# Moving the first context's rounding, the last softmax sums and the first tile's gates in a one-core pre-norm attention layer

## The reference, cut to what matters

```
h = x + attention(layernorm(x))        # 16 heads of 32, rotary q and k, causal softmax, output weights Wo
out = h + ffn(layernorm(h))
ffn(x) = x @ base_w.T + base_b + 2 * sum_e gate[e] * (x @ lora_A[e]) @ lora_B[e]   # 8 experts of rank 16
gate: softmax(x @ router_w.T + router_b), the two highest kept and divided by their sum
```

## Time and profile before

| | |
|---|---|
| median of three runs | 1532.85 us (1532.79 to 1534.3) |
| the profiled execution's own time | 1535.1 us |
| its span, first to last instruction | 1533.4 us |
| PE busy | 1503.7 us, 98% |
| DVE busy | 1134.1 us, 74% |
| ACT busy | 756.0 us, 49% |
| POOL busy | 890.6 us, 58% |
| PE's share of the chain that ended last | 91% |

### The profile page before, as it was taken

How to read it: one execution, slowest core, us unless ns; L and a number is a source line. 1 busy time by engine, 2 the same in 40 slices (tenths; PEclk the granted TensorE clock), 3 DMA queues, 4 the chain that set the end, 5 groups by cost and what they waited for, 6 DMA issues and landing times.

```text
span 1533.4 us, 24788 instructions
## 1 busy us (share of the span) xinstructions
PE 1503.7 (98%) x9056; PEld 978.2 (64%) x9056; DVE 1134.1 (74%) x2277; ACT 756.0 (49%) x1540; POOL 890.6 (58%) x597
## 2 busy tenths in 40 slices
PE   6999999999999999999999999999999989999999
PEld 5888888755555555555555555555555547777777
DVE  6766666899777877778777777877777677666665
ACT  3222222155666656657666666666665673233221
POOL 2333233567778778788788787887797721121111
PEclk9999999999999999999999999999999999999999
DMA  6656685858359457467566665754845363223411
GB/s 206 213 186 211 201 259 186 226 129 191 77 112 193 91 125 180 87 137 166 111 131 141 137 136 115 164 118 107 191 101 132 85 153 112 82 83 101 138 63 55
DMA packets 120403, 215.83 MB, mean 141 GB/s; under 512 B 12504, under 2 KB 45784, under 8 KB 113112
## 3 DMA queue, kind: packets, MB, share of 16 engines
q1 hardware_dynamic: 102384, 136.20, 32.7%
q0 software_dynamic: 8064, 58.72, 18.7%
q10 hardware_dynamic: 9840, 19.40, 3.5%
HBM read 96.23 MB, written 58.72 MB: 101 GB/s over the span
## 4 chain that ended last, share of the span: by engine, by line
PE 91%; DVE 4%; DMA 3%; issue 1%; ACT 0%; POOL 0%; SPq 0%; DVEq 0%; POOLq 0%; ACTq 0%
PE a_mx L275 17%; PE a_st L1029 17%; PE a_av L1042 16%; PE p_pair L533 11%; PE f_wo_ps L1393 5%; PE f_out_ps L1453 5%; PE p_v L545 5%; PE a_sum L275 3%; PE a_sum L1064 2%; PE a_sum L1072 2%; PE f_out_ps L1468 1%; PE f_mid_ps L1393 1%; DVE a_part L290 1%; PE a_mx L279 1%; PE f_tr_ps L1412 1%; DMA a_gather<-a_pair 1%
## 5 line engine op out<-in xcount | busy, mean ns | idle before, releaser
L1130 ACT ACTIVATE a_probs<-a_st 128x512 f32<-128x512 f32 (+2 forms) x1244 | 573.7, 547 | 344.2 <-PE a_st L1029 338.8
L290 DVE TENSOR_REDUCE a_part<-a_mx 128x1 f32<-128x512 f32 (+1 forms) x766 | 490.1, 679 | 81.7 <-PE a_mx L275 72.3
L978 POOL TENSOR_TENSOR a_pair<-a_probs 128x1024 f32<-128x1024 f32 (+2 forms) x224 | 401.4, 1832 | 18.8 <-DMA a_gather<-a_pair 6.5
L978 POOL TENSOR_TENSOR a_gather<-a_probs 128x1024 f32<-128x1024 f32 x76 | 180.0, 2388 | 94.8 <-ACT a_probs L1130 94.8
L407 POOL TENSOR_TENSOR p_rot<-p_mul 128x1024 f32<-128x1024 f32 x32 | 87.5, 2735 | 193.9 <-DVE p_mul L711 193.9
L1386 POOL TENSOR_TENSOR f_x<-f_x,f_bias 128x512 f32<-128x512 f32 x32 | 40.2, 1291 | 201.6 <-DVE f_xn L1606 201.6
L1042 PE MATMUL a_av<-a_probs,a_v 128*32 128x512 f32 (+3 forms) x1280 | 139.8, 537 | 2.3 <-POOL a_probs L959 2.3
L1042 PE MATMUL a_av<-a_probs,shared 128*32 128x512 f32 (+3 forms) x1280 | 140.1, 537 | 0.0
L293 DVE CUSTOM_DVE_ANT_0 a_mx<-a_mx,f_ctx 128x512 f32<-128x512 f32 (+1 forms) x161 | 98.5, 630 | 52.2 <-PE a_mx L275 52.2
L959 POOL TENSOR_SCALAR_AFFINE_SELECT a_probs<-a_probs 128x512 f32<-128x512 f32 x128 | 88.9, 759 | 54.8 <-ACT a_probs L1130 52.2
L1029 PE MATMUL a_st<-a_q_stack,a_k_stack 98*128 98x512 f32 (+3 forms) x287 | 101.6, 371 | 1.1 <-DMA a_q_stack<-a_neg_rows 1.1
(11 more groups left out here) (241 smaller groups left out, 3036.2 us busy)
## 6 DMA issues: line engine op xcount, KB each, us to landing
a_gather<-a_pair POOLq DMA_DIRECT2D x56, 1024.0 KB, 7.1
qk_scratch<-p_rot_hi SPq DMA_DIRECT2D x32, 512.0 KB, 3.1
qk_scratch<-p_rot_lo SPq DMA_DIRECT2D x32, 512.0 KB, 3.9
a_k_stack<-qk_scratch SPq DMA_DIRECT2D x60, 256.0 KB, 8.1
a_q_first<-qk_scratch SPq DMA_DIRECT2D x48, 256.0 KB, 6.0
a_third<-qk_scratch SPq DMA_DIRECT2D x36, 256.0 KB, 5.4
v_scratch<-p_v_st SPq DMA_DIRECT2D x32, 256.0 KB, 7.0
ctx_scratch<-a_ctx_st SPq DMA_DIRECT2D x32, 256.0 KB, 2.7
```

Of the source, the lines that this page charges most:

```text
L290: dve.tensor_reduce(found, scores.rearrange("p (h n) -> p h n", n=width), AX.X, ALU.max).then_inc(self.max_done, 1)
L978: pool.tensor_tensor(place[:, h:h + 2, q0:TT], probs[:, s % RING, h:h + 2, q0:TT], probs[:, (s + 1) % RING, h:h + 2, q0:TT], ALU.add).then ...
L1130: act.activation(probs[:, s % RING, h, q0:TT], score_bank(g, HG * s + h)[:, q0:TT], ACT.Exp, scale=SCORE_SCALE).then_inc(exp_done, 1)
```

## The change

The first context is rounded at pair 11 of the last group instead of pair 17, right behind that pair's addition. SP waits for the last join of either gather buffer before it loads the second context. PE does the sums of pair 19 behind output product 0, and waits there for the rounded output weights. In `finish` DVE does the second addition and the router weights' remainders before the second context's part; the lora_a weights' roundings and remainders come after the root and the norm. In tile 0 the logits are turned after 4 of the 12 matmuls of `down`, and the next tile's additions 0 and 1 follow the gates instead of preceding them.

```
--- before.py
+++ after.py
@@ -90,7 +90,6 @@
 ITEM_END = [max(n for n, it in enumerate(ITEMS) if it[0] == t) for t in range(QT)]
 HEAD_START = NITEM // 2 + 5
 BEFORE_FIRST = ITEM_END[1] + 1
-SPLIT_FROM = NPAIR - 7
 SHIFTS = 16 * 4
 IN_PAIRS = 5
 ITEM_AFTER = [24 * p + 4 * n + 7 for p in range(4) for n in range(IN_PAIRS)]
@@ -120,6 +119,7 @@
 
 UNIT_READY = [LAST_PAIR[t] - 1 for t in range(QT - 1)]
 OPENING = 6
+SPLIT_AT = {LAST_PAIR[2]: KT, **{LAST_PAIR[2] + 2 + n: n for n in range(KT)}}
 
 
 def items_before(p, first):
@@ -934,6 +934,8 @@
             sp.dma_start(early.x0[:, :, :], early.x_v[0]).then_inc(early.x_loaded[0], 16)
             group(GROUPS - 1, 1, False, True)
             sp.wait_ge(early.c_lo_done, 1 + START)
+            for a in range(2):
+                sp.wait_ge(gather_joined[a], 16 * joined(NPAIR * GROUPS - 1, a))
             sp.dma_start(early.cin, early.ctx_v[0, :, :, TT:2 * TT]).then_inc(early.ctx_loaded, 16)
 
         def store_last(sp):
@@ -1092,8 +1094,10 @@
                                     scores(g + 1, 1 - par, s - NSTEP, h)
                         for half in steps:
                             values(g, par, 2 * p + half)
-                    sums(g, p)
-
+                    if not (last and p == NPAIR - 1):
+                        sums(g, p)
+
+            early.last_sums = lambda: sums(GROUPS - 1, NPAIR - 1)
             pe.wait_ge(first.mul_done, 4 * TILES + PROJECT_AHEAD)
             for n in range(2 * HG):
                 scores(0, 0, n // HG, n % HG)
@@ -1159,13 +1163,12 @@
 
             def split_early(n):
 
-                if n == 0:
-                    dve.wait_ge(st_done, HG * NSTEP * (GROUPS - 1))
                 if n < KT:
                     dve.wait_ge(early.w_loaded[n], 16)
                     raw, hi, lo = early.w_raw[:, n, :], early.wo_hi[:, n, :], early.wo_lo[:, n, :]
                     hi_done, lo_done, count = early.w_hi_done, early.w_lo_done, n + 1
                 else:
+                    dve.wait_ge(st_done, HG * NSTEP * (GROUPS - 1))
                     dve.wait_ge(early.ctx_loaded, 16)
                     raw, hi, lo = early.cin, early.c_hi, early.c_lo
                     hi_done, lo_done, count = early.c_hi_done, early.c_lo_done, 1
@@ -1191,8 +1194,8 @@
                 for p in range(NPAIR):
                     if last and p >= NO_ITEMS:
                         add_pair(g, p)
-                    if last and SPLIT_FROM <= p <= SPLIT_FROM + KT:
-                        split_early(p - SPLIT_FROM)
+                    if last and p in SPLIT_AT:
+                        split_early(SPLIT_AT[p])
                     items = [(n, k) for n, k in items_of_pair(p, opening) if not (n and last)]
                     ended = [(g - before, t) for before, t in unit_ended_before(p, 1) if not (before and opening)]
                     for unit in ended:
@@ -1398,6 +1401,8 @@
                 m = 4 * T + s
                 if s == 0:
                     pe.wait_ge(c_lo_done, T + 1 + START)
+                if m == 0:
+                    pe.wait_ge(w_lo_done, KT)
                 pe.wait_ge(added, m + 1)
                 tok = slice(s * P, (s + 1) * P)
                 product(wo_ps[s % 2][:, :], [(c[u][:, kt, tok], w[:, kt, :]) for c, w in
@@ -1424,13 +1429,18 @@
                                        start=(kt == 0 and n == 0), stop=(kt == KT - 1 and n == 1))
                 mm.then_inc(router_done, 1)
 
-            def down(T, u):
-
-                pe.wait_ge(mid_copied, T + START)
-                if T == 0:
+            def down(T, u, begin=0, end=3 * KT):
+
+                if begin == 0:
+                    pe.wait_ge(mid_copied, T + START)
+                if T == 0 and begin == 0:
                     pe.wait_ge(w_lo_done, 3 * KT)
-                product(mid_ps[:, :], [(w[:, kt, :], a[:, u, kt, :]) for w, a in
-                        ((a_hi, xt_hi), (a_lo, xt_hi), (a_hi, xt_lo)) for kt in range(KT)], mid_done)
+                pairs = [(w[:, kt, :], a[:, u, kt, :]) for w, a in
+                         ((a_hi, xt_hi), (a_lo, xt_hi), (a_hi, xt_lo)) for kt in range(KT)]
+                for n in range(begin, end):
+                    mm = pe.matmul(mid_ps[:, :], *pairs[n], start=(n == 0), stop=(n == 3 * KT - 1))
+                if end == 3 * KT:
+                    mm.then_inc(mid_done, 1)
 
             def turn_logits(T):
                 wait_alone(pe, logit_copied, T + 1, pe_passed)
@@ -1471,8 +1481,10 @@
 
             def tile(T, u):
                 router(T, u)
-                down(T, u)
+                down(T, u, 0, KT if T == 0 else 3 * KT)
                 turn_logits(T)
+                if T == 0:
+                    down(T, u, KT)
                 if T > 0:
                     attention_out(T + 1, 1 - u, 0)
                     attention_out(T + 1, 1 - u, 1)
@@ -1506,7 +1518,9 @@
                 for s in range(SUB):
                     experts(T, s)
 
-            for s in range(SUB):
+            attention_out(0, 0, 0)
+            early.last_sums()
+            for s in range(1, SUB):
                 attention_out(0, 0, s)
             attention_out(1, 1, 0)
             attention_out(1, 1, 1)
@@ -1563,9 +1577,11 @@
 
             ctx_copy(1, 1)
             act.wait_ge(early.pair_done, PAIRS_DONE)
-            for n in range(KT, 3 * KT):
+            for n in range(KT, 2 * KT):
                 weights.round(act, n)
             root(0)
+            for n in range(2 * KT, 3 * KT):
+                weights.round(act, n)
             for kt in range(KT):
                 xt_copy(0, 0, kt)
             for n in range(3 * KT, 4 * KT):
@@ -1670,7 +1686,7 @@
                 gates(T)
                 if T == 0:
                     weights.rest(dve, len(jobs) - 1)
-                if more and T > 0:
+                if more:
                     add(T + 1, i + u, 1 - u, 0)
                     add(T + 1, i + u, 1 - u, 1)
                 gate_mid(T)
@@ -1691,21 +1707,20 @@
                     ctx_rest(T + 2, u)
 
             add(0, 0, 0, 0)
-            ctx_rest(1, 1)
+            add(0, 0, 0, 1)
             for n in range(KT, 2 * KT):
                 weights.rest(dve, n)
-            for s in range(1, SUB):
-                add(0, 0, 0, s)
-                weights.rest(dve, 2 * KT + s - 1)
+            ctx_rest(1, 1)
+            add(0, 0, 0, 2)
+            add(0, 0, 0, 3)
             variances(0)
             normalise(0, 0)
-            weights.rest(dve, 3 * KT - 1)
+            for n in range(2 * KT, 3 * KT):
+                weights.rest(dve, n)
             for kt in range(KT):
                 xt_rest(0, 0, kt)
             for kt in range(KT):
                 weights.rest(dve, 3 * KT + kt)
-            add(1, 0, 1, 0)
-            add(1, 0, 1, 1)
             dve.wait_ge(consts_done, 2)
             dve.wait_ge(bias_loaded, 32)
             for T in range(TILES):
```

## The result

The changed kernel takes 1541.5 us (median of 6, 1539.87 to 1542.83) against 1534.24 for the kernel before; the ratio is 1.0047, 95% interval 1.0036 to 1.0058. It is 7 us slower, where I forecast 1.1 and a range that ends at 1536.8. (The six executions of the kernel before have a median 1.4 us above the 1532.85 that the forecast started from; the time lies outside the range with that, too.) A second comparison gave 1539.97 against 1533.74, ratio 1.0038 (1.0024 to 1.0051). The profiled execution of the first took 1539.87 us with a span of 1538.1.

A forecast was written before the change was run, and what follows sets the result against it. It took PE, busy for 98% of the span, as the bound: +2.9 - 1.8 - 0.9 + 0.9 = +1.1 us on the median of 1532.85 gives 1534.0 us. Own bounds -1 and +1.4 us; with rivals 1530.8 to 1536.8.

The forecast's parts named there:

- Slide: Last group: rounding the context at pair 11 delays join 14, so PE resumes at pair 18's masks 2.9 us later.
- Recovery at addition 18: Last group: addition 18 follows its masks directly without the rounding ahead of it, so PE's 1.8 us of idle go.
- Output product: First tile: PE's 0.8 us wait for an addition goes, as the second context and addition 2 are ready in time.
- - 0.1: Up to the first tile's output product: the finer timeline's running sum, +0.2 us instead of +0.3.
- Gates: First tile: gates ahead of the next additions; shorter wait there, new waits at product (1,0) and the experts; +0.9 us.
- rival (a): Last group: the joins are not late, so the delay is absorbed; -1.7 us, 1531.1 us; chance 0.13.
- rival (b): At pair 18's masks: PE's clock falls in the longer stop; 2.3 us more, +3.4 in all, 1536.3 us; chance 0.14.
- rival (c): First tile: second context late, or last store and lora_a hold up the base weights; another 0.8, 1534.8 us; chance 0.10.

The follow-up runs named there:

- e4: Changed kernel with 14 more matmuls of unused result that keep PE busy in its stop at the masks of pair 18; +4.5 us (1.0032) against the kernel before.
- e10: Kernel before with 8 more matmuls of unused result in PE's stop at the masks of pair 18; +0.1 us (1.0000) against the kernel before.
- e5: Kernel before with only the change's first-tile part: down product split around the turned logits, next tile's additions 0 and 1 behind the gates; +1.8 us (1.0011).
- e6: As e5, but in tile 0 ACT takes the exponential before copying the down product, and DVE's addition 1 follows the gated product; -1.0 us (0.9992) against the kernel before.
- e1: Changed kernel with the first context's rounding back at pair 17; 1536.53 us against 1533.66 for the kernel before, +2.9 us (1.0017).
- e7: Kernel before with the first context's cast behind the weight piece at pair 15 and its subtraction behind the one at pair 16; +1.7 us (1.0009).
- e8: Changed kernel with the edits of e6 and e7 and SP's lora_a loads ahead of the last store; -2.2 us (0.9989) against the kernel before.
- e2: Kernel before with only the first context rounded at pair 11 and the second context's load behind the last joins; +4.2 us (1.0026).
- e3: Changed kernel with the first tile as before: down product whole, next tile's additions 0 and 1 ahead of the gates; +4.1 us (1.0026) against the kernel before.
- e11: Changed kernel with ACT's lora_a roundings ahead of the root and DVE's remainders ahead of the normalising; +6.9 us (1.0038) against the kernel before.

## Why the prediction was wrong

My sum was +2.9 - 1.8 - 0.8 - 0.1 + 0.9 = +1.1. What the stages show, step by step:

- *Slide, +2.9.* Right at its source: join 14 is 2.7 to 2.9 us late in every kernel that rounds at pair 11, and the absorbed slide, rival (a), is excluded by them. But I carried it unchanged through the queue, and PE resumes 3.8 us late. Join 15 took 10.08 us from its issue, 6.4 behind the one before instead of 5.7. In the trace's packets of the first profile after, fifteen of the sixteen engines that carry it are done by 1254.8 and one at 1256.2, and by its times that one carried a 16 KB packet of the instruction queue in between (1254.5 to 1255.4). Before, the like packet starts at 1252.0, when the join's last data is through. The 10.1 us are there in all seven profiles with the late joins; that the packet is the cause was not tried.
- *Recovery at addition 18, -1.8, and nothing for the clock.* The recovery is there, but only while the clock is up: e4 goes from +3.7 to +2.0. The clock's fall was a term of 0 in my sum. My forecast gave rival (b) 0.14 because the clock had stayed at 2.4 GHz through the stop of 2.25 us in one trace. This is the step that failed. The second profile of the same kernel has the fall behind the same stop, and the mean clocks of its executions agree (5 of 33 at 1.000, against all 11 of e10). It cost nothing there, as e10 shows, because the wait for addition 18 hid it. The change took that cover away and made the stop longer. I priced the fall at 2.3 us, and it is 1.6 to 3.2, 2.1 in the second profile; the size was right, and what was wrong is the chance and that the likeliest case left it out.
- *Output product, -0.8.* That wait was a feature of one execution (a store that landed late) and nothing that the change could win in others.
- *Base weights.* My rival (c) came true in part, and besides the forecast, not instead of it: the base loads land late behind lora_a's remainders, and PE waits 0.5 to 0.6 us for the turned logits (e5, with lora_a as before, has no such wait). ACT's timeline, after:

```profile
1289.51 1.27 ACT L218 ACTIVATE f_base_hi<-shared 128x512 fp32r<-128x512 f32 x2 [0.23 <-DMA shared<-in_base_t]
1290.69 0.57 ACT L1552 ACTIVATE f_logit_t<-f_lg_ps 16x512 f32<-16x512 f32 x1
```

- *Gates, +0.9.* The waits came where I put them (0.9, 0.5 and 1.0 us against my 0.6, 0.6 and 1.2), and the mechanism is shown by e5 and e6. The size was off, +1.65 in the stages and 1.8 by e5, and the miss is on the side of the kernel before. Counted from the first context's load, and less the 1.1 us by which PE is late in the first profile, I had the experts' operand ready at 78.1 us; in e5 it is ready at 78.1. But the wait that the part removes is 1.2 us in the second profile (and in e10) and not 1.6, and PE's start on the experts before is 0.2 us earlier than I had read it. DVE's wait for the exponential is long, but the wait at the turned logits adds nothing to it: 2.66 us in the changed kernel, 2.72 in e5, which has no such wait.

With the terms measured: +3.8 - 1.75 + 2.1 + 0.7 + 1.65 = +6.5 us, the second profile's difference, beside +6.2 in its medians. That the sum closes is no proof, as most terms are steps between stages of this profile; the experiments show the split. Of the 5.4 us that my sum lacks, the clock is 2.1, the slide's growth 0.9, the output product 0.8, the gates 0.75 and the base weights 0.7; 0.15 are in none of them. The rivals were not alternatives: (b) and (c) both happened, on top of the forecast's own mechanism, and a range made from one of them at a time ended too early. ((b)'s own upper price, 3 us on top of 1.1, would give 1536.95 and not the 1536.8 at which I ended it; that changes nothing.)

## What to carry to other kernels

A wait that a trace shows may be the name of the moment for something else: before you book its removal as a gain, ask what else holds the engine to the same time, a low clock above all. Take a second profile of the kernel before, or at least the mean clocks of its executions, before you build on single waits of under 2 us. If the idle time of an engine starts with waiting for a load, look where the load lands in it, for only the rest is free; and place work on a pacing engine where it waits for the queue that paces, not ahead of it.

## What was not expected

The granted clock can fall for 3.4 us behind a stop of PE of only 2.2 us (the second profile of before: PE resumes at 1257.4, the clock falls at 1259.1), and in one profile of the same kernel it did not. In e1, e5, e6, e7 and e8 it fell near the same place as well, for 3.4 or 6.8 us. In e2 and e3 it was low for 6.8 us behind the long stop. It also first came up at different times, from 13.3 to 20.6 us. Whether this is a part of why equal kernels scatter by 2 us is not shown: between the two profiles of the kernel before it differs by 6.5 us, and the issue of the first context's load by 0.6. In e11's profile it fell once at 34.8 us too.
